# First attention pair: four projections between the last down products, values in later slots, buffers laid out anew

## The reference

```
x = x + 0.5 * ternary_gated_network(ln(x))      # first network (f = 0)
x = x + attention(ln(x))                         # 16 heads of 128, rotary embedding
x = x + 0.5 * ternary_gated_network(ln(x))
x = x + 0.5 * experts(ln(x))
x = x + decayed_retention(ln(x))
x = x + 0.5 * experts(ln(x))
```

```
qkv = einsum('bsd,od->bso', x, w_qkv)
q, k = rope(q), rope(k)
attn = softmax(q k^T / sqrt(128));  out = (attn v) w_out
```

## Time and profile before

| | us |
|---|---|
| median of 3 runs | 1651.87 (1650.99 to 1652.86) |
| profiled execution, its own time | 1652.89 |
| span of its trace | 1651.1 |
| PE busy | 1591.3 |
| DVE busy | 1263.7 |
| ACT busy | 1214.3 |
| POOL busy | 1143.6 |

### The profile page before, as it was taken

How to read it: one execution, slowest core, us unless ns; L and a number is a source line. 1 busy time by engine, 2 the same in 40 slices (tenths; PEclk the granted TensorE clock), 3 DMA queues, 4 the chain that set the end, 5 groups by cost and what they waited for, 6 DMA issues and landing times. The chain is left out here.

```text
span 1651.1 us, 26604 instructions
## 1 busy us (share of the span) xinstructions
PE 1591.3 (96%) x9243; PEld 919.2 (56%) x9243; DVE 1263.7 (77%) x2374; ACT 1214.3 (74%) x1901; POOL 1143.6 (69%) x797
## 2 busy tenths in 40 slices
PE   3998899999999999999999999999999999999998
PEld 2566445555555555555555555555566565776665
DVE  7778787777777777777778778778787878876666
ACT  7876889989988988988988988886655433444332
POOL 0865888888888888888888888885763223663222
PEclk9999999999999999999999999999999999999999
DMA  9112789889779889879889879877004410000001
GB/s 303 51 53 48 133 153 163 142 150 183 147 144 185 149 142 185 151 142 180 153 144 173 149 140 172 147 124 145 1 2 99 119 20 1 1 1 1 1 1 52
DMA packets 621563, 183.74 MB, mean 111 GB/s; under 512 B 588779, under 2 KB 620278, under 8 KB 621174
## 3 DMA queue, kind: packets, MB, share of 16 engines
q1 hardware_dynamic: 621430, 182.04, 57.3%
HBM read 34.50 MB, written 2.10 MB: 22 GB/s over the span
## 5 line engine op out<-in xcount | busy, mean ns | idle before, releaser
L810 POOL TENSOR_TENSOR Pl<-Pm,Ph 128x1024 f16<-128x1024 f32 x256 | 545.7, 2132 | 44.5 <-ACT Ph L1105 44.1
L1651 DVE TENSOR_REDUCE nmax<-banks 128x1 f32<-128x1024 f32 x256 | 311.7, 1217 | 87.4 <-PE banks L2000 87.0
L1095 ACT ACTIVATE Pm<-banks,nbias,s_scale 128x1024 f32<-128x1024 f32 x256 | 307.4, 1201 | 96.4 <-DVE nbias L1653 95.4
L1105 ACT ACTIVATE Ph<-Pm 128x1024 f16<-128x1024 f32 x256 | 268.1, 1047 | 1.5
L789 POOL TENSOR_TENSOR rp_b<-rp_s,rope 128x512 f32<-128x512 f32 x128 | 162.8, 1272 | 99.7 <-ACT rp_s L1072 98.1
L879 POOL TENSOR_TENSOR mT_lo<-mo_h,mT_hi 128x512 f16<-128x512 f32 x72 | 83.7, 1162 | 198.5 <-ACT mT_hi L1210 198.3
L1684 DVE SCALAR_TENSOR_TENSOR X<-banks,rinv,X 128x256 f32<-128x256 f32 x256 | 112.2, 478 | 113.0 <-PE banks L2000 113.0
L1998 PE MATMUL banks<-QK_hi 128*128 128x512 f16 x512 | 194.1, 379 | 1.5 <-DVE QK_lo L1742 0.9
L1998 PE MATMUL banks<-PT_hi,V_hi 128*128 128x512 f16 x512 | 194.0, 379 | 0.4 <-DMA PT_lo<-Pl 0.4
L2000 PE MATMUL banks<-QK_hi,QK_lo 128*128 128x512 f16 x512 | 194.0, 379 | 0.0
L1999 PE MATMUL banks<-QK_lo,QK_hi 128*128 128x512 f16 x512 | 194.0, 379 | 0.0
(11 more groups left out here) (246 smaller groups left out, 4052.4 us busy)
## 6 DMA issues: line engine op xcount, KB each, us to landing
moe_raw<-in_L_ffn_W SPq DMA_DIRECT2D x48, 128.0 KB, 2.5
w_all<-in_L_attn_w_qkv SPq DMA_DIRECT2D x3, 2048.0 KB, 15.8
a_raw<-in_L_attn_w_qkv SPq DMA_DIRECT2D x24, 256.0 KB, 3.1
PT_hi<-Ph SPq DMA_TRANSPOSE x256, 3.4
PT_lo<-Pl SPq DMA_TRANSPOSE x256, 3.3
raw_gu<-in_L_ffn_w_gate_up SPq DMA_DIRECT2D x2, 1024.0 KB, 7.4
X<-in_L_attn_x SPq DMA_DIRECT2D x2, 1024.0 KB, 12.9
w_all<-in_L_attn_w_out SPq DMA_DIRECT2D x1, 2048.0 KB, 8.0
```

Source lines behind the costliest of these rows:

```text
L810: nc.gpsimd.tensor_tensor(Pl[:, z % 4, :], Pm[:, k, :], Ph[:, z % 4, :], ALU.subtract).then_inc(pl_done.sem, 1)
L1095: nc.scalar.activation(Pm[:, k, :], two_banks[z % 2][:], ACT.Exp, bias=nbias[:, z:z + 1], scale=s_scale[:], accum_out=rsum[:, z:z + 1]).th ...
L1105: nc.scalar.activation(Ph[:, z % 4, :], Pm[:, (base * SLOTS + z) % 3, :], copy).then_inc(ph_done.sem, 1)
L1651: nc.vector.tensor_reduce(nmax[:, z:z + 1], two_banks[z % 2][:], AX, ALU.max, negate=True).then_inc(max_done.sem, 1)
```

## The change

- On PE the four projections of the first head come after the second down product of the last phase and before the third and fourth. They use banks 3, 0, 1, 4 (before: 3, 0, 4, 5).
- The two values pieces that stood before the first slot become side pieces of slots 1 and 5; the third and the fourth, before in slots 1 and 6, are in slots 6 and 8. Banks and `after` of the other pieces up to slot 9 follow.
- On DVE the rotary work of the four projections (`first_ropes`) begins after the second `add` of the last phase; the third and fourth `add`, the four normalised tiles and the variance come after or among it, all before the first maximum. The fourth projection's rotary work, before in slot 1, is now ahead of the first slot, on every engine. `mean_squares` stands between the second and third `weights_lo`.
- On POOL the last `rsqrt_rms` comes before `rsqrt_ln(1, 1, 0)`, and `rsqrt_ln(1, 1, 1)` after the fourth `rp_b`.
- The attention buffers have other places in SBUF, so that `QK_hi` can be written while the network's hidden layer `hT` is still read.

```diff
@@ -259,9 +259,11 @@
     place["at"] = phase0
-    PT_hi = sb("PT_hi", [P, 2, TT, HALF], fp16)
-    PT_lo = sb("PT_lo", [P, 2, TT, HALF], fp16)
     QK_hi = sb("QK_hi", [P, 2, 2, S], fp16)
+    assert place["at"] <= hT_at
+    place["at"] = hT_at
+    Ph = sb("Ph", [P, 4, S], fp16)
     QK_lo = sb("QK_lo", [P, 2, 2, S], fp16)
+    PT_hi = sb("PT_hi", [P, 2, TT, HALF], fp16)
     V_hi = sb("V_hi", [P, 2, TT, 2 * HD], fp16)
     V_lo = sb("V_lo", [P, 2, TT, 2 * HD], fp16)
-    Ph = sb("Ph", [P, 4, S], fp16)
+    PT_lo = sb("PT_lo", [P, 2, TT, HALF], fp16)
     Pl = sb("Pl", [P, 4, S], fp16)
@@ -365,12 +367,12 @@
     SIDES["first"] = {
-        0: [Side("qk", 0, 4, 6, ("v", 0, 0))],
-        1: [Side("v", 0, 2, 7, ("v", 0, 1))],
-        2: [Side("qk", 0, 5, 6, ("qk", 0, 4))],
-        3: [Side("qk", 0, 6, 7, ("v", 0, 2))],
-        4: [Side("ln", 1, 0, 6, ("qk", 0, 5))],
-        5: [Side("ln", 1, 1, 7, ("qk", 0, 6))],
-        6: [Side("v", 0, 3, 6, ("ln", 1, 0))],
-        7: [Side("ln", 1, 2, 7, ("ln", 1, 1)), Side("qk", 0, 7, 6, ("v", 0, 3))],
-        8: [Side("qk", 1, 0, 7, ("ln", 1, 2))],
-        9: [Side("ln", 1, 3, 6, ("qk", 0, 7))],
+        0: [Side("qk", 0, 4, 7, ("add", 0, 2))],
+        1: [Side("v", 0, 0, 6, ("add", 0, 1))],
+        2: [Side("qk", 0, 5, 7, ("qk", 0, 4))],
+        3: [Side("qk", 0, 6, 6, ("v", 0, 0))],
+        4: [Side("ln", 1, 0, 7, ("qk", 0, 5))],
+        5: [Side("v", 0, 1, 6, ("qk", 0, 6))],
+        6: [Side("ln", 1, 1, 7, ("ln", 1, 0)), Side("v", 0, 2, 6, ("v", 0, 1))],
+        7: [Side("ln", 1, 2, 7, ("ln", 1, 1)), Side("qk", 0, 7, 6, ("v", 0, 2))],
+        8: [Side("qk", 1, 0, 7, ("ln", 1, 2)), Side("v", 0, 3, 6, ("qk", 0, 7))],
+        9: [Side("ln", 1, 3, 6, ("v", 0, 3))],
         10: [Side("qk", 1, 1, 6, ("ln", 1, 3)), Side("v", 1, 0, 7, ("qk", 1, 0))],
@@ -862,5 +864,4 @@
                         pool.wait_ge(rope_sum.sem, pre(rope_sum, j - 1))
-                    if j == 3:
-                        rsqrt_ln(1, 1, 1)
                     rope_sine(j, pre, PRE_QKO)
+                rsqrt_ln(1, 1, 1)
                 attention_pair("first", 0)
@@ -1151,4 +1152,2 @@
                         exponentials(s)
-                    if body == "first" and s == 1:
-                        rope_hi(3, of(rope_sum, 4))
                     for side in SIDES[body][s]:
@@ -1174,10 +1173,9 @@
                 act.wait_ge(rope_b.sem, pre(rope_b, 1))
-                rope_shift_step(2, bank[4], pre(qk_psum, 3))
+                rope_shift_step(2, bank[1], pre(qk_psum, 3))
                 rope_hi(0, pre(rope_sum, 1), PRE_QKO)
-                values_hi(0, 0, bank[6], pre(v_psum, 1))
+                act.wait_ge(rope_b.sem, pre(rope_b, 2))
+                rope_shift_step(3, bank[4], pre(qk_psum, 4))
                 rope_hi(1, pre(rope_sum, 2), PRE_QKO)
-                values_hi(0, 1, bank[7], pre(v_psum, 2))
                 rope_hi(2, pre(rope_sum, 3), PRE_QKO)
-                act.wait_ge(rope_b.sem, pre(rope_b, 2))
-                rope_shift_step(3, bank[5], pre(qk_psum, 4))
+                rope_hi(3, pre(rope_sum, 4), PRE_QKO)
                 attention_pair("first", 0)
@@ -1595,11 +1593,14 @@
                         weights_lo(W_ORDER[i], bank[i], w_hi_done.in_head(0, i + 1))
-                    gate_weights_split()
+                        if i == 1:
+                            mean_squares(len(PHASES) - 1)
                     ln_variance(1, l + 1, 0)
+                    gate_weights_split()
+                    add(len(PHASES) - 1, 0)
+                    add(len(PHASES) - 1, 1)
+                    first_ropes(add)
                 else:
                     expert_weights_lo(1)
-                mean_squares(len(PHASES) - 1)
-                for j in range(TPH):
-                    add(len(PHASES) - 1, j)
-                    if f == 0 and j == 1:
-                        ln_normalise(1, l + 1, 0)
+                    mean_squares(len(PHASES) - 1)
+                    for j in range(TPH):
+                        add(len(PHASES) - 1, j)
 
@@ -1693,7 +1694,2 @@
                         maximum(s)
-                    if body == "first" and s == 0:
-                        values_lo(0, 1, bank[7], of(v_hi_done, 2))
-                    if body == "first" and s == 1:
-                        rope_cos(3, bank[5], of(rope_shift, 8), PRE_QKO)
-                        rope_add(3, bank[5], of)
                     if body == "tail" and block_done(s, body):
@@ -1748,10 +1744,17 @@
                 rope_add(1, bank[0], pre)
-                rope_cos(2, bank[4], pre(rope_shift, 6), PRE_QKO)
+                rope_cos(2, bank[1], pre(rope_shift, 6), PRE_QKO)
                 rope_lo(0)
                 dve.wait_ge(qk_lo.sem, pre(qk_lo, 1))
-                rope_add(2, bank[4], pre)
+                rope_add(2, bank[1], pre)
                 rope_lo(1)
+                rope_cos(3, bank[4], pre(rope_shift, 8), PRE_QKO)
                 rope_lo(2)
-                values_lo(0, 0, bank[6], pre(v_hi_done, 1))
+                add(len(PHASES) - 1, 2)
+                dve.wait_ge(qk_lo.sem, pre(qk_lo, 2))
+                rope_add(3, bank[4], pre)
+                add(len(PHASES) - 1, 3)
+                ln_normalise(1, 1, 0)
                 ln_variance(1, 1, 1)
+
+            def attention():
                 attention_pair("first", 0)
@@ -2155,2 +2158,4 @@
                         pe.wait_ge(h_ready.sem, h_ready.in_head(f, NS))
+                    if f == 0 and j == 2:
+                        first_projections()
                     down(len(PHASES) - 1, j)
@@ -2234,2 +2239,4 @@
                         pe.wait_ge(v_lo_done.sem, of(v_lo_done, i + 1, d))
+                    elif name == "add":
+                        pe.wait_ge(x_added.sem, x_added.before(0, 1) - 3 + i)
                     elif name == "ln":
@@ -2289,6 +2296,3 @@
 
-            def attention():
-                def pre(sig, i):
-                    return sig.in_pair(0, i)
-
+            def first_projections():
                 x_ready(0, 1, 0)
@@ -2299,10 +2303,11 @@
                 x_ready(0, 1, 1)
+                project(0, 2, bank[1], PRE_QKO)
                 pe.wait_ge(x_added.sem, x_added.before(0, 1) - 3)
-                project(0, 2, bank[4], PRE_QKO)
-                pe.wait_ge(x_added.sem, x_added.before(0, 1))
-                pe.wait_ge(w_lo_done.sem, w_lo_done.in_head(0, 3))
-                values(0, 0, bank[6])
-                values(0, 1, bank[7])
-                project(0, 3, bank[5], PRE_QKO)
+                project(0, 3, bank[4], PRE_QKO)
+
+            def attention():
+                def pre(sig, i):
+                    return sig.in_pair(0, i)
 
+                pe.wait_ge(w_lo_done.sem, w_lo_done.in_head(0, 3))
                 pe.wait_ge(qk_lo.sem, pre(qk_lo, 2))
```

More of the change, by code:

```diff
@@ L259, in build_program @@
     place["at"] = phase0
+    QK_hi = sb("QK_hi", [P, 2, 2, S], fp16)
+    assert place["at"] <= hT_at
+    place["at"] = hT_at
+    Ph = sb("Ph", [P, 4, S], fp16)
+    QK_lo = sb("QK_lo", [P, 2, 2, S], fp16)
     PT_hi = sb("PT_hi", [P, 2, TT, HALF], fp16)
-    PT_lo = sb("PT_lo", [P, 2, TT, HALF], fp16)
-    QK_hi = sb("QK_hi", [P, 2, 2, S], fp16)
-    QK_lo = sb("QK_lo", [P, 2, 2, S], fp16)
     V_hi = sb("V_hi", [P, 2, TT, 2 * HD], fp16)
     V_lo = sb("V_lo", [P, 2, TT, 2 * HD], fp16)
-    Ph = sb("Ph", [P, 4, S], fp16)
+    PT_lo = sb("PT_lo", [P, 2, TT, HALF], fp16)
     Pl = sb("Pl", [P, 4, S], fp16)
@@ L781, in ffn @@
                         nc.gpsimd.tensor_tensor(l_root[:], l_norm[:], neg_half[:, 0:3], ALU.pow).then_inc(l_rooted.sem, 1)
+                rsqrt_rms(len(PHASES) - 1)
                 if f == 0:
                     rsqrt_ln(1, l + 1, 0)
-                rsqrt_rms(len(PHASES) - 1)
             def rope_sine(j, c, order=QKO):
@@ L839, in attention_pair @@
                             rope_lo(side.i, lambda sig, i, d=side.d: of(sig, i, d))
+                    if s == 0 and body == "first":
+                        rope_lo(3, of)
                     if s and has_slots(body):
@@ L844, in attention_pair @@
                     if has_slots(body):
-                        if s == 1 and body == "first":
-                            rope_lo(3, of)
                         for side in sides_of(s - 3) if body != "first" or s < SLOTS - 1 else []:
@@ L1595, in ffn @@
                         weights_lo(W_ORDER[i], bank[i], w_hi_done.in_head(0, i + 1))
+                        if i == 1:
+                            mean_squares(len(PHASES) - 1)
+                    ln_variance(1, l + 1, 0)
                     gate_weights_split()
-                    ln_variance(1, l + 1, 0)
+                    add(len(PHASES) - 1, 0)
+                    add(len(PHASES) - 1, 1)
+                    first_ropes(add)
                 else:
                     expert_weights_lo(1)
-                mean_squares(len(PHASES) - 1)
-                for j in range(TPH):
```

(8 more changed lines are left out.)

## The result

The changed kernel takes 1661.28 us, median of 6 executions (1656.99 to 1663.16), against 1651.51 us (1650.84 to 1652.86, 6 executions) for the kernel before on the same chip: ratio 1.0056, 95% interval 1.0044 to 1.0068. By the medians it is slower by 9.8 us, by the ratio 9.2, where 6.0 were forecast, and the median lies 0.8 us above the range. The profiled execution took 1660.34 us with a span of 1658.6 us, 7.5 more than before.

A forecast was written before the change was run, and what follows sets the result against it. PE, busy 1591.3 of 1651.1 us, bounds the kernel. Front gain spent, slots 1 to 5 come 0.45 us earlier, bank 6 waits make slot 11 6.15 late: sum +6.0, forecast 1657.9 us, range 1654.0 to 1660.5.

The forecast's parts named there:

- the range: Forecast range of the changed kernel's time, 1654.0 to 1660.5 us, taking in the partly hidden case and the clock.
- The front: Before slot 0: PE starts scores some 3.5 us earlier, but DVE work keeps the first maximum at 150.8; gain spent.
- The weighed rule: Front, DVE waiting for a whole POOL instruction: second `QK_lo` would wait for the fourth `rp_b`, some 0.3 us more.
- Slots 1 to 5: One `QK_hi` less on ACT in slot 1: slots come 0.45 us earlier, maximum of slot 6 at 171.5.
- Slots 6 to 10: Pieces in bank 6 wait on one another through DVE: scores of slot 11 start 6.15 us late, +6.0 us in time.
- the link of slot 6: Third values piece waits for the second's `V_lo` in bank 6: scores of slot 7 3.15 us late.
- the term for the clock: PE in slots 2 to 9: no lower-clock loss in the sum; as rival, chance 0.05, 1660.3.
- the bounds: Alternatives around the +6.0 us sum: +4.9 without the front's clock dip, +7.3 with late first maximum, +8.4 with more clock lost.
- up to 1.1 us more: Bound for PE, idle half of slots 2 to 9, getting the lower clock for one stretch; total +8.4.
- a late first maximum: Bound: first maximum late by one whole POOL instruction of the `rp_b` kind, 1.3 us; total +7.3.

The follow-up runs named there:

- Experiment 3: Changed kernel's front on all engines, but first two values pieces before slot 0 and the side-piece table of before: 1650.96 us, ratio 0.9997 to the kernel before.
- experiment 1: Kernel before with only the buffer places of the changed kernel: 1651.33 us against 1651.23, ratio 1.0001.
- experiment 6: Changed kernel with 51 extra matmuls, results unread, put where PE waited: 1657.66 us, ratio 1.0036 to the kernel before.
- experiment 2: Kernel before with its own front and buffers but the changed kernel's table of side pieces: 1660.88 us, ratio 1.0057.
- experiment 5: Changed kernel with second values piece in bank 4, third in bank 5, second ln piece in slot 5, bank 6: 1654.82 us, ratio 1.0026 to before.
- experiment 4: Changed kernel with the second values piece in bank 5 instead of 6: 1658.22 us, ratio 1.0040 to the kernel before.
- experiment 7: Changed kernel with extra matmuls only at the end of slot 1 (11) and before slot 6's third values piece (10): 1660.87 us, ratio 1.0056 to before.
- experiment 8: Changed kernel's front, first two values pieces made before exponential 0, other side pieces spread over banks 4 to 7: 1651.41 us, ratio 0.9996 to before.
- experiment 9: Kernel of early values pieces, with four normalised tiles and variance moved behind the second maximum on DVE: 1653.71 us, ratio 1.0013 to the kernel before.

## Why the prediction was right in its mechanism and too low in its size

- **The front**: `rp_s` at 137.51 (137.6), first maximum at 150.72 (150.8), PE's wait 2.81 us (some 3). Experiment 3 shows that the lead is spent, by a gain of nothing. Both times are right in part by luck: the projection starts at 135.65, 0.6 later than I took, but the clock is back up 0.9 us sooner than 137.2, and the two cancel; the last `QK_lo` ends at 146.46 (146.25), and the block behind it takes 4.3 us (4.5). I took the low clock there as given, since what PE does before it is unchanged; but seven of the eleven traces don't have it, and without it everything behind is some 1.4 us earlier, in the kernel before (experiment 1) as in the changed one (experiment 6).
- **The weighed rule**: the second `QK_lo` took 1.16 us beside POOL's `rp_b` (143.41 to 144.71) and the third 0.68 beside none, 0.48 us more for the estimated 0.3. The trace agrees with the rule in the Trainium skill (SBUF — State Buffer, "Who interferes with whom"). The first maximum did not come later for it, so it is no part of the miss.
- **Slots 1 to 5**: maximum of slot 6 at 171.45 (171.5).
- **Slots 6 to 10**: right. Experiments 2 and 3 put the loss into the table of side pieces; experiment 5 takes the link of slot 6 out and about half of the loss with it, which experiment 4 alone doesn't show; experiment 6, with the clock held, gives 6.0 us at slot 11 and 6.2 in the span for the forecast 6.15 and 6.0. Two details are off. In slot 7 PE waited first, for 0.87 us, for the low part of the `ln` piece in bank 7, a wait that the prediction doesn't have; it costs nothing, for the projection started when its own `V_lo` let it, as forecast. And of the pieces before, the third projection of the second head (slot 3) used bank 7; bank 6 had the second one, in slot 2.
- **The step that failed** is the term for the clock. The sum has it at nothing for slots 2 to 9. The prediction put it in the bounds, as "up to 1.1 us more" for one stretch, with a chance of 0.05, and its 1660.3 for that case also counts a late first maximum that had no part in it; the clock alone would have given 1659.0. In the profiled execution there were two stretches, behind the waits of 2.81 and 2.33 us; from maximum 0 to maximum 11 it took 200.11 - 150.72 = 49.39 us against 197.00 - 149.29 = 47.71 with the waits filled, so 1.7 us. Over all executions it is 3.6 us in the median (1661.28 - 1657.66), and the two ends of experiment 7 are 8.4 apart (1665.81 - 1657.37), with the low clock ahead of slot 0 in the slower. The prediction gives no reason for the small chance. The earlier trace rows show a clock of 1.00 in this stretch, but those are rows of a PE with 7.9 us of idle time there, and the forecast itself made it some 14.
- What stays open is how many such stretches an execution gets and how long they are: in experiment 7 the same program ran with a mean clock of 1.00 and with three such stretches, and no row says which it will be. The 3.6 us of experiment 6 come from medians of two comparisons; by their ratios (1.0056 and 1.0036) it is 0.2%, 3.3 us, and as the two intervals (1.0044 to 1.0068, 1.0023 to 1.0048) touch, it may be much less or more.

## What to carry to other kernels

A piece that waits for its bank stands ahead of the scores that the next maximum needs, and what frees the bank stands behind that maximum: two neighbours in one bank turn such an order into a chain, so give them different banks first (experiment 8), and then ask what the moved work itself costs in its new slot. When a change is forecast to add waits of 2 us and more to PE, price the lower clock behind them as likely, more than once, and expect a spread between executions. A lead won on one engine is worth what the fullest engine behind it leaves (ACT in experiment 8): read that engine's windows first.

## What was not expected of the hardware

- In the changed kernel and in experiments 2, 4, 5, 7 and 9, PE has waits of 2.0 to 3.6 us from slot 0 on, and one to three of them were followed by a granted clock of 0.50; which ones changed from program to program. Filling the waits with 51 matmuls whose results nobody reads held it at 1.00 and made the median 3.6 us lower.
- Not each long wait has this behind it, and the stretches are not alike: in the changed kernel they run from about 153 to 157 and from 174 to 177 us, in experiment 5 from 154 to 160 and from 167 to 174. Where only one wait in the slots was over 2 us, of 2.47 us (before) and of 2.04 us (experiment 8), the clock stayed at 1.00.
- The ten executions of one program (experiment 5) fall into two groups 4.5 us apart (1653.9 to 1655.1 against 1658.2 to 1660.3), and the mean granted clock parts them in the same way. Only a slow one has a trace, with 0.86 from 150 to 200 us, so that the clock alone makes the difference is likely but not shown. The kernel before, with one wait over 2 us, stays within 3.1 us over 21 executions on the chip of experiments 1 to 4 (1650.70 to 1653.78).
